# One more recurrence tick in the expert stage, and another order of work inside each tick

## The reference

```python
x = x + GLA(LN(x)) * silu(FFN0(LN(x)))     # layer 0
x = x + MHA(LN(x)) * silu(FFN1(LN(x)))     # layer 1
```

## Time and profile before

| | |
|---|---|
| median of 3 runs | 975.24 us (974.64 to 975.46) |
| the profiled execution, its own time | 974.64 us |
| its span, first to last instruction | 972.8 us |
| busy share of the span: PE, DVE, ACT, POOL | 74%, 67%, 63%, 46% |
| scatter stage with ticks 1 to 7 | 45 to 158.1 us |
| expert stage, steps 0 to 11 (ticks 8 to 15) | 158.1 to 308.2 us |
| expert stage, from step 12 until the output of group 16 | 308.2 to 358.5 us |

### The profile page before, as it was taken

The page is one execution under the profiler, slowest core; times in us unless marked ns, Lnnn a source line. Parts: engine busy times, 40 slices in busy tenths (PEclk is TensorE's granted clock), DMA queues, the critical chain, the costliest instruction groups (busy, mean ns, idle before and its releaser), DMA issues.

```text
span 972.8 us, 20676 instructions
## 1 busy us (share of the span) xinstructions
PE 718.9 (74%) x7862; PEld 557.4 (57%) x7862; DVE 653.0 (67%) x1206; ACT 610.6 (63%) x1137; POOL 446.0 (46%) x468
## 2 busy tenths in 40 slices
PE   6757778898898970686927676787888888888660
PEld 4545557788788860454714444565666666666540
DVE  5777776776776536767575544476687688688547
ACT  6653656866866544674613343676878788788775
POOL 5475773233343462000006655223666666656632
PEclk8767998999999995777965778798999999999885
DMA  9811212011111217000005222200111111111063
GB/s 310 316 44 44 85 53 56 25 54 46 30 49 45 58 42 206 1 1 1 2 1 192 75 74 86 56 15 26 40 34 40 39 35 39 42 32 29 18 175 107
DMA packets 62355, 63.77 MB, mean 66 GB/s; under 512 B 7378, under 2 KB 52322, under 8 KB 62132
## 3 DMA queue, kind: packets, MB, share of 16 engines
q1 hardware_dynamic: 53300, 44.02, 15.5%
q0 software_dynamic: 8960, 18.43, 5.8%
HBM read 31.88 MB, written 30.55 MB: 64 GB/s over the span
## 4 chain that ended last, share of the span: by engine, by line
PE 23%; ACT 15%; DVE 15%; issue 9%; another core or an unknown queue 2%; POOL 1%; DMA 1%; SPq 0%; ACTq 0%; DVEq 0%
ACT arena L1227 5%; PE bank L710 4%; PE bank L775 3%; PE bank L787 3%; ACT L870 2%; PE bank L680 2%; DVE arena L1660 2%; DVE arena L1753 2%; ACT arena L1128 2%; DVE arena L1640 1%; PE bank L789 1%; DVE arena L1658 1%; PE bank L748 1%; DVE arena L1741 1%
## 5 line engine op out<-in xcount | busy, mean ns | idle before, releaser
L1912 POOL DMA_INDIRECT ys<-arena x152 | 163.8, 1078 | 214.5 <-DVE arena L1624 79.0
L1893 POOL DMA_INDIRECT xs<-arena x128 | 133.5, 1043 | 84.0 <-issue 31.3
L1227 ACT ACTIVATE arena<-bank 128x512 f32<-128x512 f32 x192 | 99.0, 601 | 83.2 <-PE bank L775 59.6
L1753 DVE TENSOR_REDUCE arena<-bank 128x2 bf16<-128x512 f32 (+1 forms) x192 | 119.2, 683 | 41.8 <-PE bank L748 34.0
L650 PE MATMUL bank<-arena 128*128 128x128 bf16 x608 | 105.9, 220 | 20.6 <-DVE arena L1605 14.0
L651 PE MATMUL bank<-arena 128*128 128x128 bf16 x608 | 105.9, 220 | 0.0
L652 PE MATMUL bank<-arena 128*128 128x128 bf16 x608 | 105.8, 219 | 0.0
L1741 DVE SCALAR_TENSOR_TENSOR arena<-arena,bank 128x512 bf16<-128x512 bf16 x64 | 46.0, 746 | 72.2 <-ACT arena L1200 64.9
L870 ACT ACT_TABLE_LOAD x70 | 89.8, 1283 | 1.2
L650 PEld LDWEIGHTS bank<-arena 128*128 x608 | 59.0, 97 | 25.4 <-issue 14.4
L710 PE MATMUL bank<-arena 128*128 128x256 f32 x256 | 68.3, 415 | 0.9 <-issue 0.9
(11 more groups left out here) (232 smaller groups left out, 1976.0 us busy)
## 6 DMA issues: line engine op xcount, KB each, us to landing
xs<-arena SPq DMA_DIRECT2D x19, 516.0 KB, 7.5
arena<-xs SPq DMA_DIRECT2D x38, 258.0 KB, 2.9
arena<-ys SPq DMA_DIRECT2D x32, 256.0 KB, 5.1
arena<-in_MF SPq DMA_DIRECT2D x8, 512.0 KB
ys<-arena POOLq DMA_INDIRECT x152
arena<-in_x SPq DMA_DIRECT2D x8, 256.0 KB, 5.6
arena<-in_W SPq DMA_DIRECT2D x8, 256.0 KB
xs<-arena POOLq DMA_INDIRECT x128
```

What stands on the lines that cost most here:

```text
L1227: act(PT[kt_][:, i, gs[0]:gs[0] + len(gs), :], bank_of["s2", b, n, i][:, :].rearrange("p (g q) -> p g q", q=w), ACT.Exp, scale=8 ** -0.5). ...
L1753: red(negM[b % 2][:, u, 32 * i + gs[0]:32 * i + gs[0] + len(gs)], kv_, op=ALU.max, negate=True).then_inc(m_max.sem, 1)
L1893: eng.indirect_dma_start(xs[l][:, :], bass.IndirectOffsetOnAxis(ap=slot_i[l][:, m:m + 1], axis=0), xrow[:, t, :], None).then_inc(rows_move ...
L1912: eng.indirect_dma_start(ys[l][:, :], bass.IndirectOffsetOnAxis(ap=yid[g % 4][:, j:j + 1], axis=0), y[:, 128 * j:128 * j + 128], None).the ...
```

## The change

OUTPUTS_EARLY goes from 8 to 7 and TICKS gets tick 7 in front: ticks 1 to 6 stay in the scatter stage, whose 64 transfers are cut into 18 portions, and 13 ticks run in the 19 steps of the expert stage. Ticks 17, 18 and 19 now stand in neighbouring steps. Inside the ticks of the expert stage the work is ordered anew:

- PE: `output_means(t-4)` and `gate_out(t)` go to the head of part 0, in front of the scores.
- ACT: `outputs_scale(t-4)` goes to the head of part 0; `gate_sizes` and `gate_logs` are one function again, in part 0 behind `crossed` and in front of the tanh; `decays(t-1)` is the first of part 1; `outputs_squared` and `chunk_hi` go to part 2, and where the next step has a tick too, EXP_LN is loaded there.
- DVE: `gate_sigmoids(t)` is in part 1 of its own tick, behind `chunk_lo`; the scan `decays(t)` is the last work of the tick, behind `scaled` and `keys_shifted`, from t = 6 on.
- POOL: the store in part 0 waits for `o_mean` instead of `att`. `output_gates` stays in part 0.

```diff
-OUTPUTS_EARLY = 8
-TICKS = (8, 9, 0, 10, 11, 0, 12, 13, 0, 14, 15, 0, 16, 0, 17, 0, 18, 19, 0)
+OUTPUTS_EARLY = 7
+TICKS = (7, 8, 9, 0, 10, 11, 0, 12, 13, 0, 14, 15, 0, 16, 0, 17, 18, 19, 0)
...
-            for t in range(1, 8):
+            for t in range(1, 7):
                 for part in range(3):
-                    do["scatter"](0, 3 * (t - 1) + part, 21)
+                    do["scatter"](0, 3 * (t - 1) + part, 18)
...
             def gla(t, part):                                   # PE
                 if part == 0:
-                    if at(t - 4) and t <= OUTPUTS_EARLY:
+                    if at(t - 4):
                         output_means(t - 4)
-                    if at(t) and not beside:
+                    if at(t):
                         gate_out(t)
-                    if at(t - 2) and beside:
+                    if at(t - 2) and t >= OUTPUTS_EARLY:
                         scores(t - 2)
                 elif part == 1:
-                    if at(t - 3) and beside:
+                    if at(t - 3) and t >= OUTPUTS_EARLY:
                         outputs(t - 3)
-                    if at(t) and beside:
-                        gate_out(t)
...
-                    if at(t - 3) and beside:
-                        output_means(t - 3)
...
             def gla(t, part):                                   # ACT
                 if part == 0:
-                    if at(t - 4) and t <= OUTPUTS_EARLY:
+                    if at(t - 4):
                         outputs_scale(t - 4)
-                    if at(t - 2) and beside:
+                    if at(t - 2) and t >= OUTPUTS_EARLY:
                         crossed(t - 2)
-                    if at(t) and not beside:
-                        gate_sizes(t)
+                    if at(t):
                         gate_logs(t)
                 elif part == 1:
...
-                    if at(t - 1) and not beside:
+                    if at(t - 1):
                         decays(t - 1)
-                    if at(t - 3) and beside:
-                        outputs_squared(t - 3)
-                    if at(t) and beside:
-                        gate_sizes(t)
                     if at(t + 1):
                         gate_moved(t + 1)
                     if at(t - 1):
                         values_moved(t - 1)
...
+                else:
+                    if at(t - 3):
+                        outputs_squared(t - 3)
+                    if at(t):
                         chunk_hi(t)
...
+                    if t in TICKS and t + 1 in TICKS[TICKS.index(t):TICKS.index(t) + 2]:
+                        table(EXP_LN)
                     if at(t - 4):
                         attended(t - 4)
...
             def gla(t, part):                                   # DVE
                 if part == 0:
-                    if at(t - 1) and not beside:
+                    if at(t - 1) and t < OUTPUTS_EARLY:
                         decays(t - 1)
...
-                    if at(t - 1) and t > OUTPUTS_EARLY:
-                        gate_sigmoids(t - 1)
                 elif part == 1:
...
-                    if at(t - 1) and beside:
-                        chunk_lo(t - 1)
-                        decays(t - 1)
                     if at(t + 1):
                         gate_low(t + 1)
...
-                    if at(t - 1) and not beside:
+                    if at(t - 1):
                         chunk_lo(t - 1)
-                    if at(t) and not beside:
+                    if at(t):
                         gate_sigmoids(t)
                 else:
                     if at(t - 1):
                         scaled(t - 1)
                         keys_shifted(t - 1)
+                    if at(t) and t + 1 >= OUTPUTS_EARLY:
+                        decays(t)
...
             def experts0(g, part):                              # POOL
-                    eng.wait_ge(*(att.at(t - 2, 0) if 0 < t < 18 else up[0].at(g, 1) if g < 18 else down[0].at(17)))
+                    eng.wait_ge(*(o_mean.at(t - 4) if t else up[0].at(g, 1) if g < 18 else down[0].at(17)))
```

More of the change, by code:

```diff
@@ L320, in walk @@
                 do["gla"](0, part)
-            for t in range(1, 8):
+            for t in range(1, 7):
                 for part in range(3):
-                    do["scatter"](0, 3 * (t - 1) + part, 21)
+                    do["scatter"](0, 3 * (t - 1) + part, 18)
                     do["gla"](t, part)
-                    if part == 0 and 3 <= t < 7:
+                    if part == 0 and 3 <= t:
                         do["w1"](2 * t - 6)
@@ L330, in walk @@
                     do["route_end"](0, t // 2)
-                if 3 <= t < 7:
+                if 3 <= t:
                     do["w1"](2 * t - 5)
@@ L557, in at @@
                     return 0 <= b < NB
-                beside = t >= OUTPUTS_EARLY
                 if part == 0:
-                    if at(t - 4) and t <= OUTPUTS_EARLY:
+                    if at(t - 4):
                         output_means(t - 4)
-                    if at(t) and not beside:
+                    if at(t):
                         gate_out(t)
-                    if at(t - 2) and beside:
+                    if at(t - 2) and t >= OUTPUTS_EARLY:
                         scores(t - 2)
                 elif part == 1:
-                    if at(t - 3) and beside:
+                    if at(t - 3) and t >= OUTPUTS_EARLY:
                         outputs(t - 3)
-                    if at(t) and beside:
-                        gate_out(t)
-                    if at(t - 2) and not beside:
+                    if at(t - 2) and t < OUTPUTS_EARLY:
                         scores(t - 2)
@@ L577, in gla @@
                 else:
-                    if at(t - 3) and not beside:
+                    if at(t - 3) and t < OUTPUTS_EARLY:
                         outputs(t - 3)
-                    if at(t - 3) and beside:
-                        output_means(t - 3)
                     if at(t - 1):
@@ L1064, in gla @@
                         values_moved(t - 1)
-                    if at(t) and beside:
+                else:
+                    if at(t - 3):
+                        outputs_squared(t - 3)
+                    if at(t):
                         chunk_hi(t)
-                    if at(t - 1) and beside:
-                        decays(t - 1)
-                else:
-                    if at(t - 3) and not beside:
-                        outputs_squared(t - 3)
-                    if at(t) and not beside:
[L1073 to L1077, removed]
+                    if t in TICKS and t + 1 in TICKS[TICKS.index(t):TICKS.index(t) + 2]:
+                        table(EXP_LN)
                     if at(t - 4):
@@ L1572, in at @@
                     return 0 <= b < NB
-                beside = t >= OUTPUTS_EARLY
                 if part == 0:
-                    if at(t - 1) and not beside:
+                    if at(t - 1) and t < OUTPUTS_EARLY:
                         decays(t - 1)
-                    if at(t - 2) and beside:
+                    if at(t - 2) and t >= OUTPUTS_EARLY:
                         masked(t - 2)
-                    if at(t - 4) and beside:
+                    if at(t - 4) and t >= OUTPUTS_EARLY:
                         gated(t - 4)
-                    if at(t - 1) and t > OUTPUTS_EARLY:
-                        gate_sigmoids(t - 1)
                 elif part == 1:
-                    if at(t - 2) and not beside:
+                    if at(t - 2) and t < OUTPUTS_EARLY:
                         masked(t - 2)
-                    if at(t - 1) and beside:
-                        chunk_lo(t - 1)
-                        decays(t - 1)
                     if at(t + 1):
                         gate_low(t + 1)
-                    if at(t - 4) and not beside:
+                    if at(t - 4) and t < OUTPUTS_EARLY:
                         gated(t - 4)
-                    if at(t - 1) and not beside:
+                    if at(t - 1):
                         chunk_lo(t - 1)
-                    if at(t) and not beside:
+                    if at(t):
                         gate_sigmoids(t)
```

8 lines of the change are left out of this document (2 added, 6 removed).

## The result

The changed kernel takes 1000.41 us (median of 4 runs, 996.82 to 1001.39), the kernel before 974.94 us on the same chip (972.23 to 975.46): ratio 1.0261, 95% interval 1.0228 to 1.0292. Slower, as forecast, but by 25.5 us where I had 11.1, and outside the range that ended at 996. The profiled execution took 999.84 us, its span is 998.0 us (972.8 before), the mean granted clock 0.867 (0.874 before).

The account below looks back on a forecast made before the run. It took one serial chain through PE, ACT and DVE to bound tick steps. Start 145.2, steps 182.7 and end 41.7 gave 369.6 against 358.5, 11.1 us longer: 974.6 + 11.1 + 0.6, forecast 986 us, range 976 to 996.

Parts of the forecast that it names:

- The bound of a tick step: Expert stage, full tick steps: one serial chain, PE 4.2, ACT 8.4, DVE 4.1, makes each 16.7 us; chance 0.72.
- The first rival: Expert stage: PE stays the bound, steps keep 14.9 us per tick and 7.7 without, kernel 968 us; chance 0.12.
- the second (gain and loss cancel): Expert stage: a chain of 15.3 to 15.7 us per tick gives a kernel of 973.5 to 977 us; chance 0.06.
- The plain step: Expert stage, step without a tick behind a tick: DVE's scan delays `lo`, so 8.1 us instead of 7.7.
- The table switch: ACT's chain in a tick step: a switch costs its 1.28 us load alone, without the skill's drain of about 1380 ns.
- The early table load worth nothing: ACT, expert stage ticks: the new early load moves nothing, as `outputs_scale` ends before 4.17 us either way.
- the changed wait of POOL worth nothing: POOL's store in part 0 waits for `o_mean`, which is early in the step, so it costs nothing.
- The end: Expert stage from step 12 on, until group 16's rows are done: 41.7 us instead of 50.3, bounds 40.8 and 44.7.
- The start (part 1): Scatter stage without tick 7: PE starts the expert stage at about 145.2 instead of 158.1, 12.9 us gained.
- the waits cost more than the chain: PE, expert stage: idling lowers the clock in a quarter of the ticks, POOL 3 us later, kernel 1000 us; chance 0.10.
- the last rival: Rival that PE's waits bring 1.2 GHz in a quarter of the expert stage's ticks, kernel 1000 us; chance 0.10.
- rival three: Rival of low PE clock in a quarter of the expert stage's ticks and POOL 3 us later, 1000 us; chance 0.10.

Follow-up runs that it names:

- the copy beside it: Changed kernel plus one unneeded 128x1024 ACT copy ahead of `chunk_hi` in part 2, ticks 7 to 15, off the chain: 1005.94 us, ratio 1.0244.
- a copy put on the chain: Changed kernel plus one unneeded 128x1024 ACT copy ahead of `crossed`, ticks 7 to 17: 1015.25 us, ratio 1.0337 to the kernel before.
- filled: Changed kernel with useless bf16 matmuls of 128x512 where PE waits in the expert stage: 956.43 us, ratio 1.0190 to the kernel before.
- the logs here: Changed kernel with `gate_logs` moved behind `chunk_hi` in part 2 and `gate_sigmoids` behind `keys_shifted`: 954.58 us, ratio 1.0192 to the kernel before.
- the filled kernel before: Kernel before with eight useless fp32 matmuls of 128x512 ahead of PE's wait for `xq_lo`: 933.92 us, ratio 0.9960; on the third chip 934.86 us, 0.9975.

## Why the prediction was wrong

By its own sum, 145.2 + 182.7 + 41.7 = 369.6 predicted and 383.5 measured:

- **The bound of a tick step.** Right, and shown: 16.7 predicted, 16.72 to 16.80 in every step of ticks 8 to 14 at a clock of 1.00, in the six runs whose chain is the changed kernel's or has the copy beside it, on four chips; link by link within 0.1 us; longer by a copy put on the chain, not by the same copy beside it. Tick 15, which I had counted as the ninth full one, takes 15.6 us: no gate copy for a next sequence stands in it. The first rival (PE stays the bound, 968) and the second (gain and loss cancel) fall with it.
- **The plain step.** 8.1 predicted, 8.08 measured behind a full tick step where the clock is 1.00; 7.4 behind tick 15.
- **The table switch.** No drain, as the row of before had said.
- **The early table load worth nothing, the changed wait of POOL worth nothing.** Not tested alone.
- **The end.** 41.7 predicted, 42.6 measured: +0.9.
- **The start (part 1).** 145.2 predicted, 150.4 measured: +5.2. The count of POOL's instructions held, 64 at 1.10 us. What failed is the sum in which POOL never waits for a tick ("with POOL free of waits"): it had five waits for the ticks, 6.3 us in all, and the last ticks of the scatter stage were slow on this chip. Whether the 18 portions for 21 have a part in it isn't shown. On the second and third chips the stage starts at 143.2 (filled) and 145.8. The size hangs on the chip; my bound (+3) was too narrow for this one.
- **The first step and the later dips.** This is the step that failed. I costed the first tick step like the others, with no term for the lower clock, and gave "the waits cost more than the chain" 0.10. The first step took 22.2 us (+5.5) at a clock of 0.77: 1.7 and 2.7 us of it are the lower clock at its head and tail, 1.1 is the second transposition, which I had left out. The last four steps with or between gates (9.7, 17.4, 15.6 and 9.0 us, the first two in the rows above at 0.82 and 0.90) took 2.1 us more than their 49.6. Against the same steps at 1.00 the lower clock costs 1.6, 0.6 and 1.6 us in three of them, and 1.1 and 0.7 come off, since tick 15 and the plain step behind it are shorter than I had them. So the lower clock costs about 8.2 us in all.

5.2 + 5.5 + 2.1 + 0.9 and 0.2 in the other steps are 13.9, and with the 11.1 of the forecast 25.0 of the 25.2 us by which the span grew.

What was wrong in the argument is the row that I set against the last rival: a tick in the scatter stage with PE busy 11.5 of 14.7 us at a clock of 1.00. A busy share over a whole step says nothing of how its idle time is cut. In the first step of the expert stage it is two waits, of 2.27 and 2.23 us; in the tick step that keeps the clock it is 1.98 and 0.4; with the copy on the chain the first alone became 2.7, and the clock fell in every tick step. The length of a wait isn't all of it, either. Two plain steps of the changed kernel have the same wait in the same place:

```profile
210.96 0.22 PE L645 MATMUL bank<-arena 128*128 128x128 bf16 x1 [2.16 <-DVE arena L1580]
...
294.13 0.22 PE L645 MATMUL bank<-arena 128*128 128x128 bf16 x1 [2.16 <-DVE arena L1580]
```

The first of the two ran at 1.00 and took 8.0 us, the second at 0.82 and took 9.7. The kernel thus stands at an edge at which the clock sometimes holds and sometimes doesn't; which of the two it will be, no run here tells. It is the changed order that brought it there: in the first three tick steps of the kernel before no wait of PE is longer than 0.91 us, the old order with the moved tick keeps its 15.3, 14.7 and 7.7 us to tick 15, and the new order alone has the long steps. I had 3.3 us of PE's idle time in the sum, and should have laid them out as waits, each with its length and place, and priced the lower clock where they stood together. The Trainium skill, "TensorE: Matmul & The Clock Gate", section "Loop structure matters more than you think", ties the clock to idle spells in the loop. The longest in the expert stage of before is 1.7 us, and the clock is 1.00 there; the trace of after has those of 2.0 to 2.3 us ahead of its falls, and agrees.

The close match of rival three's 1000 us with 1000.41 is partly luck: it had 11 us of low clock spread over a quarter of the ticks and 3 us of start; it was 8.2 us, half of it in one step, and 5.2.

**What stays open.** Why the ticks at the end of the scatter stage are slow on some chips. On the chip of the result, consumers of PE's results waited long after PE's records had ended, for a releaser that the profile can't name ("remote"); two rows of the changed kernel, the second from PE's timeline:

```profile
116.18 0.38 ACT L1029 ACTIVATE arena<-bank 128x256 f32<-128x256 f32 x1 [5.90 <-remote]
...
111.79 0.39 PE L552 MATMUL bank<-arena 128*128 128x128 f32 x2
```

From one `gate_out` to the next (114.2 to 134.0, 19.8 us) the same tick took 13.4 us on the third chip (113.1 to 126.6). That scatters' traffic slows the ticks was not tried: without the scatters the experts' rows are undefined.

## What to carry over

Ordering every engine's work by first use can tie three engines into one chain: count a step once as the largest busy time and once as the longest path from the bank that is freed to the bank that is needed next, and take the larger. Then lay out TensorE's idle time in that step wait by wait: waits of 2.0 us and more stood ahead of each fall of the clock that was followed up here (and ahead of stretches that kept it), and each fall cost another 0.6 to 2.7 us. A work item moved off a chain (the logs here) must be followed into the next step of every kind, the short one too.

## What was not expected of the hardware

- Useless matmuls shortened a step: nine of 128x512 in a plain step took it from 9.7 to 8.0 us; with eight in the kernel before its time was 0.25 to 0.4% less.
- The same kernel takes 938.3, 938.9, 974.9 and 980.3 us on different chips. Tick steps of PE without slack differ (13.4 us in the filled kernel before, 14.6 in the unfilled one on the chip of the result), chains across three engines don't (16.7 on all).
- A table load stood on the chain with 1.28 us and a gap of 0.02; taken off, it gave 1.4.
